# Attention block on one core: three PSUM banks take turns for value products and row maxima, and the maxima are turned with a transpose

## What is computed

```python
xs = jnp.reshape(x, (B, T, C))                       # x here: after the group norm
q = jnp.einsum('btc,hcd->bhtd', xs, Wq)
k = jnp.einsum('btc,hcd->bhtd', xs, Wk)
v = jnp.einsum('btc,hcd->bhtd', xs, Wv)
scores = jnp.einsum('bhtd,bhsd->bhts', q, k) * scale
att = jax.nn.softmax(scores, axis=-1)
out = jnp.einsum('bhts,bhsd->bhtd', att, v)
out = out @ Wproj + bproj
x = x + _L0_conv_ref(_gn(x), ...)
```

## Time and profile before

| | |
|---|---|
| median of three runs | 4950.16 us |
| profiled execution, from the first to the last instruction | 4946.9 us |
| lowest and highest of the runs | 4949.59 and 4951.74 us |
| PE busy | 4705.1 us, 95% |
| ACT busy | 2886.6 us, 58% |
| DVE busy | 2775.5 us, 56% |
| POOL busy | 2326.6 us, 47% |
| mean granted TensorE clock | 0.994 of full |

### The profile page before, as it was taken

One profiled execution on the slowest core, in us unless ns is written; L12 is line 12 of the kernel. 1 busy time (PEld: TensorE's weight loads), 2 busy tenths in 40 slices (PEclk: granted clock), 3 DMA queues, 4 the chain that ended last, 5 costly groups with the idle time before them and its releaser, 6 DMA issues.

```text
span 4946.9 us, 73065 instructions
## 1 busy us (share of the span) xinstructions
PE 4705.1 (95%) x20608; PEld 3505.4 (71%) x20608; DVE 2775.5 (56%) x5284; ACT 2886.6 (58%) x5507; POOL 2326.6 (47%) x1837
## 2 busy tenths in 40 slices
PE   7999999999999999999999999999999999999998
PEld 5777767777676776767767677676776767767675
DVE  5655646556465564655646556465564655646454
ACT  4665646556465564655646566464664646656465
POOL 2444545445454454544545445454444545445455
PEclk9999999999999999999999999999999999999999
DMA  2111111111111111111111111211112111111101
GB/s 69 34 37 55 31 53 35 46 46 32 52 34 50 43 34 54 31 53 41 32 54 35 51 41 30 63 28 53 37 30 62 35 49 35 32 61 34 53 23 51
DMA packets 156934, 212.71 MB, mean 43 GB/s; under 512 B 56544, under 2 KB 57568, under 8 KB 156512
## 3 DMA queue, kind: packets, MB, share of 16 engines
q1 hardware_dynamic: 156512, 207.47, 15.0%
HBM read 105.12 MB, written 34.08 MB: 28 GB/s over the span
## 4 chain that ended last, share of the span: by engine, by line
issue 50%; POOL 42%; PE 6%; POOLq 1%; ACT 1%; DVE 0%; DMA 0%; SPq 0%; ACTq 0%; DVEq 0%
POOL prob_l L1031 32%; POOL o L1048 6%; POOL res L1054 3%; PE bank L517 1%; PE bank L561 1%; POOLq L1030 1%; POOL rstd L1023 1%; PE bank L578 1%; PE bank L690 1%; PE bank L692 1%; PE bank L691 1%; PE bank L571 0%; PE bank L572 0%; POOLq L1047 0%; DMA xs<-in_x 0%
## 5 line engine op out<-in xcount | busy, mean ns | idle before, releaser
L1031 POOL TENSOR_TENSOR prob_l<-prob,prob_h 128x512 fp32r<-128x512 f32 x1408 | 1803.5, 1288 | 2470.5 <-ACT prob_h L710 2452.6
L710 ACT ACTIVATE prob<-bank 128x512 f32<-128x512 f32 x2048 | 1237.6, 604 | 1698.6 <-PE bank L572 1579.3
L864 DVE TENSOR_REDUCE smax<-bank 128x1 f32<-128x512 f32 x2048 | 1349.1, 684 | 1012.6 <-PE bank L578 997.8
L710 ACT ACTIVATE prob_h<-bank 128x512 fp32r<-128x512 f32 x2048 | 1236.7, 604 | 198.6 <-PE bank L692 154.9
L690 PE MATMUL bank<-prob_h,vh 128*128 128x512 f32 x2048 | 832.6, 407 | 117.9 <-ACT acc L781 99.3
L578 PE MATMUL bank<-k_hl,q_hh 128*128 128x512 f32 x2048 | 802.5, 436 | 33.6 <-DVE smax L864 30.4
L571 PE MATMUL bank<-q_hh,k_hl 128*128 128x512 f32 x2048 | 824.0, 402 | 0.5 <-ACT prob_h L710 0.5
L572 PE MATMUL bank<-q_lm,k_h 65*128 65x512 f32 x2048 | 813.8, 397 | 0.0
L692 PE MATMUL bank<-prob_l,vh 128*128 128x512 f32 x2048 | 809.6, 395 | 0.0
L691 PE MATMUL bank<-prob_h,vl 128*128 128x512 f32 x2048 | 809.0, 395 | 0.0
L803 DVE TENSOR_TENSOR prob_l<-prob,prob_h 128x512 fp32r<-128x512 f32 x640 | 508.0, 804 | 511.9 <-ACT prob_h L710 511.8
(11 more groups left out here) (58 smaller groups left out, 4393.2 us busy)
## 6 DMA issues: line engine op xcount, KB each, us to landing
xs<-in_x SPq DMA_DIRECT2D x128, 256.0 KB, 2.8
q_hh<-q_hh SPq DMA_DIRECT2D x256, 128.0 KB, 2.2
k_hl<-k_h SPq DMA_DIRECT2D x256, 128.0 KB, 2.4
inv_b<-inv_dram SPq DMA_DIRECT2D x256, 128.0 KB, 2.8
res<-in_x SPq DMA_DIRECT2D x128, 256.0 KB, 2.7
out_x<-res SPq DMA_DIRECT2D x128, 256.0 KB, 2.0
q_lm<-q_lm SPq DMA_DIRECT2D x256, 2.0 KB
den<-acc SPq DMA_DIRECT2D x256, 2.0 KB, 1.7
```

Source lines behind the costliest of these rows:

```text
L710: return nc.scalar.activation(out, ps[ST + bank][:, :], ACT.Exp, scale=SCALE)
L864: nc.vector.tensor_reduce(smax[:, j:j + 1], ps[SM + j % 2][:, :], AX.X, ALU.max).then_inc(rows_used, 1)
L1031: nc.gpsimd.tensor_tensor(prob_l[:, r3, :], prob[:, ring2, :], prob_h[:, r3, :].bitcast(F32), ALU.subtract).then_inc(prob_l_pool, 1)
```

## The change

Three banks (TURN, 3 to 5) replace SM and PVB. The value sum of a half head takes the bank that VALUE_BANK lists for it, so that two value sums in a row lie in different banks, and row products take whichever of the other two was used least recently. In place of the wait for `acc_ready` ahead of slots 0 and 8 and of the wait for row j - 2 stands `turn_free`: it waits for whoever used that bank last, a row maximum of DVE (`rows_used`) or a copy of ACT (`acc_ready`); where the bank had no user in this head, it waits until all row maxima of the steps so far are taken. `turns` works out these users when the kernel is built. The row products are issued by `other_rows`, now behind the value product in every slot, so that in slots 0 and 8 they move from ahead of it to behind it. Each "mt" is a `transpose` with the identity in place of a matmul with it. All engines' orders are otherwise the same.

```diff
-ST, SM, PVB, WB = 0, 3, 5, 6
+ST, TURN, WB = 0, 3, 6
+VALUE_BANK = (0, 1, 2, 0, 1, 2, 0, 1, 2, 0, 1, 2, 0, 1, 2, 1)
...
+def turns(h, per_slot):
+    user = [None, None, None]
+    row_turn, value_turn = [], []
+    age = {b: -1 for b in range(3)}
+    user[VALUE_BANK[2 * h - 1]] = ("value", -1)
+    for i in range(BLOCKS):
+        tc, t = divmod(i, 8)
+        value, after = VALUE_BANK[2 * h + tc], VALUE_BANK[(2 * h + tc + 1) % BLOCKS]
+        if t == 0:
+            value_turn.append(user[value])
+            user[value] = ("value", tc)
+            if tc:
+                age[VALUE_BANK[2 * h]] = 2 * i
+        for n in range(per_slot[i], 0, -1):
+            late = t == 7 and n == 1
+            bank = min((b for b in range(3) if b != value and not (late and b == after)),
+                       key=lambda b: (t != 7 or b != after, age[b]))
+            row_turn.append((bank, user[bank]))
+            user[bank] = ("row", len(row_turn) - 1)
+            age[bank] = 2 * i + 3 - n
+    return row_turn, value_turn
...
+        def turn_free(eng, s, user):
+            if user is None:
+                eng.wait_ge(rows_used, s.heads(BLOCKS, 1))
+            elif user[0] == "row":
+                eng.wait_ge(rows_used, s.heads(BLOCKS, 1, user[1] + 1))
+            elif not (s.section == "first" and user[1] < 0):
+                eng.wait_ge(acc_ready, s.heads(2, 0, user[1] + 1))
...
-                    nc.tensor.matmul(w[0:4, 0:P], nmax[:, a * 4:(a + 1) * 4], ident[:, :],
-                                     start=True, stop=True).then_inc(mt_done, 1)
+                    nc.tensor.transpose(w[0:4, 0:P], nmax[:, a * 4:(a + 1) * 4], ident[:, :]).then_inc(mt_done, 1)
...
-                    pe.wait_ge(rows_used, s.heads(BLOCKS, 1, j - 1))
-                    row_scores((s.k + 1) % 2, j)
+                    bank, user = s.row_turn[j]
+                    turn_free(pe, s, user)
+                    row_scores((s.k + 1) % 2, j, bank)
...
-                    if t == 0 and not (first and tc == 0):
-                        pe.wait_ge(acc_ready, s.heads(2, 0, tc))
+                    if t == 0:
+                        turn_free(pe, s, s.value_turn[tc])
...
-                    bank = PVB
+                    bank = TURN + VALUE_BANK[2 * s.h + tc]
...
                     if i not in s.first[0]:
                         other_work(s, i)
+                    other_rows(s, i)
...
-                nc.scalar.copy(acc[:, tc, :], ps[PVB][:, :]).then_inc(acc_ready, 1)
+                nc.scalar.copy(acc[:, tc, :], ps[TURN + VALUE_BANK[2 * s.h + tc]][:, :]).then_inc(acc_ready, 1)
```

More of the change, by code:

```diff
@@ L190, in __init__ @@
         self.looped = section == "body"
+        self.row_turn, self.value_turn = turns(
+            self.h, max_blocks(self.h, self.has_next, self.looped and k == 8))
     def at(self, per_batch, const):
@@ L573, in scores, with row_scores @@
                                  start=False, stop=True).then_inc(scores_ready, 1)
-            def row_scores(slot, j):
+            def row_scores(slot, j, turn):
                 t, half = divmod(j, 2)
-                nc.tensor.matmul(ps[SM + j % 2][:, :], q_hh[:, slot, t * P:(t + 1) * P],
+                nc.tensor.matmul(ps[TURN + turn][:, :], q_hh[:, slot, t * P:(t + 1) * P],
                                  k_hl[:, slot, half * 512:(half + 1) * 512], start=True, stop=True).then_inc(rows_ready, 1)
@@ L613, in _ @@
                     pe.wait_ge(rows_used, j - 1)
-                row_scores(0, j)
+                row_scores(0, j, j % 2)
                 if j == 9:
@@ L644, in other_work, with other_rows @@
                     entry(kind, a, lo, hi, bk, before, (s.h + (2 if kind == "qn" else 1)) % NH, wait)
+            def other_rows(s, i):
                 per_slot = max_blocks(s.h, s.has_next, s.section == "body" and s.k == 8)
@@ L860, in take, with take_max @@
                     last.then_inc(taken[bank], 1)
-            def take_max(j, count):
+            def take_max(j, count, turn):
                 dve.wait_ge(rows_ready, count)
-                nc.vector.tensor_reduce(smax[:, j:j + 1], ps[SM + j % 2][:, :], AX.X, ALU.max).then_inc(rows_used, 1)
+                nc.vector.tensor_reduce(smax[:, j:j + 1], ps[TURN + turn][:, :], AX.X, ALU.max).then_inc(rows_used, 1)
             def combine(half, used):
@@ L908, in _ @@
                     for j in range(10, BLOCKS):
-                        take_max(j, j + 1)
+                        take_max(j, j + 1, j % 2)
                     combine(1, BLOCKS)
@@ L944, in maxima @@
                         for _ in range(per_slot[i - 1] if i else 0):
-                            take_max(hj, s.heads(BLOCKS, 1, hj + 1))
+                            take_max(hj, s.heads(BLOCKS, 1, hj + 1), s.row_turn[hj][0])
                             hj += 1
```

## The result

The kernel with the change takes 5055.0 us (5049.5 to 5060.0), beside 4951.0 us for the kernel before on the same chip: ratio 1.0209, 95% interval 1.0195 to 1.0224. It is 104 us slower. The forecast was 5069 us.

What follows compares the result with a forecast made beforehand. PE bounds the kernel, busy 4705 of 4946.9 us. A batch loses 6.2 (slot 0) - 1.2 (slot 8) - 1.3 (turn) + 4.0 (clock) = 7.7 us; times 15.5 that is 119 us, giving 5069 us, range 4997 to 5110.

Steps and rivals of the forecast that it cites:

- Slot 0: First value product of each head waits for DVE's last row maxima instead of ACT's copy: 6.2 us lost a batch.
- Head 1's start: Maxima there are taken long before the value product; no gain expected, 0, at best 1.1 us earlier.
- Slot 8: Value product no longer waits for the copy: 0.38, 0.38 and 0.44 in heads 1, 2, 7; 1.2 us gained a batch.
- The turn: Turn of the maxima (L557) needs one pass less on PE: 0.11 us each, 12 a batch, 1.3 us gained.
- The rival in which the turn costs almost nothing: Turn as a transpose saves 0.38 us in place of 0.11: 50 us less than forecast, 5019 us; chance 0.10.
- The clock at the starts: PE's clock falls after longer idle at four more head starts, two times in three, 1.5 us each: 4.0 us a batch.
- "Nothing else": Beyond row products moved in slots 0 and 8 and waits moved or replaced, no other effect of the change; no cost given.
- The faster case: DVE's last maxima aren't late, so the copy's wait is saved: 110 us, with the turn 130, 4820 us; chance 0.08.

Runs made afterwards that it cites:

- The kernel with the wait alone: Kernel before, own banks and order, plus one PE wait at slot 0 until all row maxima so far are taken: 5137.2 us, ratio 1.039.
- the kernel with the filler: Kernel after, with five never-read matmuls on PE ahead of the slot 0 wait in heads 2, 3 and 4: 5012.0 us, ratio 1.0119.
- the kernel that removes them: Kernel after, with two small products of the token statistics on DVE reading one input from PSUM: 4999.9 us, ratio 1.0104.

## Why the prediction was right, and where its steps were not

The forecast, 5069 us, is 14 us above the measured median, and the sign and the reason hold: the wait for the copy is replaced by a later one for the maxima. That it came so near is luck in part: the turn was 70 us too small and a loss of 50 us wasn't foreseen, in opposite directions.

- **Slot 0: right in its mechanism and size.** The product starts 0.13 us behind the maxima, as said. Longer idle time from the turn-only kernel to the kernel after, forecast in brackets: head 0 0.57 (0.56), head 2 1.54 (1.54), head 3 1.54 (1.54), head 4 1.53 (1.53), head 5 0.80 (0.79), head 6 0.80 of which 0.59 comes back in slot 2 (0.2), head 7 none (0). The kernel with the wait alone shows the cause.
- **Head 1's start: near for the banks, missed for the turn.** Its 1.12 us of idle time are gone. But the kernel with the turn alone already has 0.29 in their place, with the product 0.13 us behind the copy in place of 0.94, and its slot is 0.45 shorter; the banks add 0.1. So the 0.94 was not the copy, as I said, but not untouched by the change either. What it was the profile doesn't show, and I did not try.
- **Slot 8: right.** From the turn-only kernel to the kernel after 0.38, 0.37 and 0.28 are gained in heads 1, 2 and 7 (0.38, 0.38, 0.44). In heads 4 and 5 it gains 0.3 and loses as much in slot 9, as argued. In head 6 slots 7 to 9 add up to nothing: +1.80, -1.13, -0.68.
- **The turn: mis-sized, 0.11 against 0.39 us.** The step that failed is "take away one pass, 0.11 us" (the working beside it gives 0.12); its upper bound, 2 x 0.19 = 0.38, lies just below what was measured. It went by PE's busy time of the records, and a hold-up of the neighbours is in their start times, not in that. In the trace of before the distance from L692 to L572 at a turn, 0.98 us against 0.46, was there to be read: 0.52 a turn. With it and the transposes at 0.12 the term would have been 0.40 x 12 x 15.5 = 74 us in place of 20. The rival in which the turn costs almost nothing was right as a mechanism. The remaining 16 us of the 90 are mostly head 1's start (0.45 us a batch) and fewer falls at head 0 (0.65), which no term of the sum had.
- **The clock at the starts: right in size, by luck in its counts.** Forecast were 4 more starts x 2/3 x 1.5 = 4.0 us a batch. Falls came in 15, 13, 9 and 0 batches of heads 2 to 5, so 37 of some 60 in place of 40; the kernel with the filler prices one at 1.5 us. That every start falls in two batches of three was wrong, and no such rate holds: with the banks alone the same starts, with the same idle times, fell in 9, 12, 3 and 12.
- **Head 3, slot 9: not foreseen.** "Nothing else" was the step that failed. The wait and the fall behind it are 3.33 us a batch from the turn-only kernel to the kernel after, 50 us; the kernel that removes them shows the cause. The prediction asked what is late next only at slots 0 and 8, and not where DVE, now at another phase against POOL, meets it.
- **The sum.** Banks: forecast 139 us (6.2 - 1.2 + 4.0, x 15.5), measured 5055.0 - 4860.7 = 194 on top of the turn (191 without it), of which 50 are head 3's slot 9, so 144 without them. Turn: forecast -20, measured -90 alone. 139 - 20 = 119 and 194 - 90 = 104.
- **The faster case,** 4820 us if the last maxima aren't late, is close to the kernel with earlier row products and statistics in PSUM, 4823.6. But it had the price of its parts wrong: 89 us of it come with the turn, 38 with the banks.

## What to carry to other kernels

Before a buffer is freed from one reader by giving it to several users, look at when its new last user's reader is through, and at what stands in that reader's queue: here the same change went from 104 us slower to 87 us faster by issuing the last row products one or two slots earlier. Take a change apart before you praise it: these 87 us are the turn's 90, the banks came out even with them (4864.1 beside 4860.7 us), and they gave 38 us only once the statistics read from PSUM too. Read the price of a small instruction from the start times of its neighbours, not from its own duration. And when a wait grows on TensorE, price the slower matmuls behind it along with the wait.

## What the runs showed of the hardware

- An fp32 matmul of 128 x 4 by 128 x 128, two records, takes 0.52 us out of a run of 512-column matmuls; the same as a transpose, one record, takes 0.12 us.
- A DVE operation of 128 x 4 with both inputs in SBUF takes 0.16 us alone and up to 1.27 us beside POOL's 128 x 512 operations, and ends within 0.02 us of POOL's; with one input in PSUM it takes 0.14 to 0.17 us at the same place.
- After 2.4 us of idle time at a head's start TensorE was granted 1.2 GHz in 15 of 16 batches in head 2, after 1.9 us in 9, after 2.0 us in head 5 in none, and after 1.23 us, with five filling matmuls ahead of it, in none. With the banks alone and the same idle times it was 9, 3 and 12 of 16. A fall costs 1.5 us. What decides besides the idle time wasn't found.
- A row product that waits for a DMA starts 0.09 us after its landing; the copy of k_h takes 2.4 us from issue to landing (median of 256).
